# A gated recurrence and a mixture of experts on one core: who computes the convolution, and where the gates of two chunks stand

## What is computed

```python
xn = layernorm(x)
# branch 1: gated linear recurrence
xc = causal_depthwise_conv(xn, conv_w, conv_b)      # 4 taps along a sequence
r, i = sigmoid(xc @ W_r.T + b_r), sigmoid(xc @ W_i.T + b_i)
a = sigmoid(log_a) ** (8 * r)
h[t] = a[t] * h[t-1] + sqrt(max(1 - a*a, 0)) * (i * xc)[t]
attn = rmsnorm(h @ W_out.T) * gamma
# branch 2: 8 experts, one per token, at most 512 tokens each
probs = softmax(xn @ Wr);  e = argmax(probs)
slot = number of earlier tokens with the same e;  keep = slot < 512
y[token] = probs[e] * keep * (relu(xn[token] @ W1[e]) @ W2[e])
out = x + attn + y
```

## Time and profile before

| what | us |
|---|---|
| median of 3 runs | 165.67 (165.46 to 167.71) |
| the profiled execution, its own time | 165.59 |
| its span, first to last instruction | 163.8 |
| PE busy | 124.8 |
| DVE busy | 93.5 |
| ACT busy | 86.2 |
| POOL busy | 83.2 |

### The profile page before, as it was taken

The page is one execution under the profiler, slowest core; times in us unless marked ns, Lnnn a source line. Parts: engine busy times, 40 slices in busy tenths (PEclk is TensorE's granted clock), DMA queues, the critical chain, the costliest instruction groups (busy, mean ns, idle before and its releaser), DMA issues.

```text
span 163.8 us, 2058 instructions
## 1 busy us (share of the span) xinstructions
PE 124.8 (76%) x684; PEld 98.2 (60%) x684; DVE 93.5 (57%) x207; ACT 86.2 (53%) x197; POOL 83.2 (51%) x102
## 2 busy tenths in 40 slices
PE   5966999999995991699999739896979967941000
PEld 5956999836533890439659318694968956930000
DVE  4179300399898000861512410768948999299990
ACT  3047625014554840648685363999608958635650
POOL 7069640000477774377477876377765807560000
PEclk9997555579999999569999999999999999999555
DMA  4898699970011211011011111011110100116997
GB/s 133 231 270 315 268 356 342 399 318 2 16 48 36 54 58 48 18 49 49 16 52 48 48 48 48 16 50 49 49 46 21 33 16 32 42 58 183 327 301 214
DMA packets 14346, 19.27 MB, mean 118 GB/s; under 512 B 1664, under 2 KB 10112, under 8 KB 14336
## 3 DMA queue, kind: packets, MB, share of 16 engines
q1 hardware_dynamic: 9888, 13.63, 24.5%
q0 software_dynamic: 2048, 4.20, 8.7%
q10 hardware_dynamic: 2400, 1.32, 3.0%
HBM read 10.76 MB, written 8.39 MB: 117 GB/s over the span
## 4 chain that ended last, share of the span: by engine, by line
PE 40%; DVE 24%; DMA 8%; issue 8%; ACT 7%; another core or an unknown queue 6%; POOL 3%; POOLq 1%; SPq 0%; DVEq 0%; ACTq 0%
PE bank L495 8%; PE bank L427 7%; PE bank L385 7%; DVE xnT L869 5%; DMA x_tok<-in_x 4%; PE bank L395 4%; DVE xc L838 4%; PE bank L482 3%; DVE inp L865 3%; PE bank L416 3%; PE bank L484 2%; PE bank L483 2%; DVE dec L922 2%; DMA dec<-y_rows 2%
## 5 line engine op out<-in xcount | busy, mean ns | idle before, releaser
L357 POOL DMA_INDIRECT y_rows<-xn_tok,idx_out x32 | 37.1, 1159 | 25.2 <-DVE xn_tok L876 15.9
L350 POOL DMA_INDIRECT xn_tok<-xn_rows,idx_in x32 | 32.1, 1002 | 29.9 <-DVE idx_out L801 20.4
L618 ACT ACTIVATE h_sb<-bank 128x512 f32<-128x512 f32 x32 | 18.1, 596 | 25.7 <-PE bank L484 16.8
L495 PE MATMUL bank<-w_raw,h_sb 128*128 128x128 f32 x256 | 30.2, 275 | 0.1
L495 PEld LDWEIGHTS bank<-w_raw,h_sb 128*128 128x128 f32 x256 | 29.2, 192 | 0.2 <-issue 0.2
L482 PE MATMUL bank<-xg_hi,w_hi 128*128 128x512 f32 x32 | 14.0, 437 | 12.0 <-ACT h_sb L618 5.4
L427 PE MATMUL bank<-xc,par 128*128 128x512 f32 x32 | 17.2, 670 | 3.0 <-issue 2.8
L845 DVE TENSOR_TENSOR xg_lo<-bank,xg_hi 128x512 fp32r<-128x512 f32 x8 | 5.5, 688 | 18.6 <-ACT xg_hi L612 14.2
L876 DVE COPY xn_tok<-bank 128x512 f32<-128x512 f32 x7 | 4.8, 684 | 18.2 <-remote 11.3
L482 PEld LDWEIGHTS bank<-xg_hi,w_hi 128*128 128x128 f32 x32 | 6.1, 191 | 14.9 <-ACT h_sb L618 6.8
L427 PEld LDWEIGHTS bank<-xc,par 128*128 128x128 f32 x32 | 6.6, 214 | 12.0 <-issue 11.0
(11 more groups left out here) (111 smaller groups left out, 211.8 us busy)
## 6 DMA issues: line engine op xcount, KB each, us to landing
w_raw<-in_weights SPq DMA_DIRECT2D x8, 512.0 KB, 7.5
y_rows<-sca SPq DMA_DIRECT2D x4, 512.0 KB, 5.8
dec<-y_rows SPq DMA_DIRECT2D x8, 256.0 KB, 5.0
x_tok<-in_x SPq DMA_DIRECT2D x3, 512.0 KB, 9.4
xn_rows<-xn_tok SPq DMA_DIRECT2D x3, 512.0 KB, 3.5
out<-dec SPq DMA_DIRECT2D x4, 256.0 KB, 3.0
out<-dec ACTq DMA_DIRECT2D x4, 256.0 KB, 3.2
x_tok<-in_x SPq DMA_DIRECT2D x2, 256.0 KB, 5.4
```

Of the source, the lines that this page charges most:

```text
L350: g.indirect_dma_start(gathered[:, s * D:(s + 1) * D], None, xn_rows, bass.IndirectOffsetOnAxis(ap=idx_in[:, s:s + 1], axis=0)).then_inc(g ...
L357: g.indirect_dma_start(y_rows, bass.IndirectOffsetOnAxis(ap=idx_out[:, s:s + 1], axis=0), gathered[:, s * D:(s + 1) * D], None).then_inc(s ...
L495: last = mm(tile_of(e, s), h_sb[:, k * CAP + s * P:k * CAP + (s + 1) * P], w_raw[:, e, F + k * D:F + (k + 1) * D], start=(k == 0), stop=(k ...
L618: a(h_sb[:, k * CAP:(k + 1) * CAP], hbank[n % 3][:, :], ACT.Relu).then_inc(h_done, 1)
```

## The change

- PE no longer convolves and POOL no longer builds the diagonal matrices; `biased` is gone from ACT. DVE convolves all four chunks: chunks 0 and 1 before `untile(7)`, chunk 2 at the place of half 3, chunk 3 after `columns_rest(0)`.
- `gates(0)` stands on PE where the first half of conv 0 stood, before the counts, and `gates(1)` between counts and table. PE has nothing between the table and `turn(0)`. `gates(2)` and `gates(3)` stand in the turns of experts 0 and 1, and the turn of expert 2 has no gates.
- ACT computes Ln and loads the table set for exp before the routing, then the tanh of gates(0), then the exp of the logits, `lead(0)`, `lead(1)`, the tanh of gates(1), and decay(0) before `columns(0)`. decay(1) to decay(3) stand one turn earlier each.
- The three small instructions of DVE for `lna` move to behind `untile(7)`, ahead of the routing. gated and clip keep their turns but for those of chunk 2, which move from turn 3 to turn 2.

```diff
--- before.py
+++ after.py
...
-        diag = sb("diag", [P, TAPS, P])
...
-        PE_CONV = 3
...
-        def convolved(eng, n):
-
-            if n < PE_CONV:
-                eng.wait_ge(conv_act, n + 1)
-            else:
-                eng.wait_ge(conv_dve, TAPS * (1 + (n - PE_CONV + 1) // 2))
-
-        PE_AFTER_TABLE = "gates0"
+        def convolved(eng, c):
+
+            eng.wait_ge(conv_dve, TAPS * (c + 1))
+
         PE_AT = {5: "project0", 7: "project6 project7"}
-        PE_AFTER = {0: "gates1", 1: "gates2", 2: "gates3", 5: "project1 project2", 6: "project3 project4 project5"}
-        ACT_AT = {0: "decay0", 1: "decay1", 2: "decay2", 3: "decay3", 4: "scale1 scale2 scale3",
+        PE_AFTER = {0: "gates2", 1: "gates3", 5: "project1 project2", 6: "project3 project4 project5"}
+        ACT_AT = {0: "decay1", 1: "decay2", 2: "decay3", 4: "scale1 scale2 scale3",
                   6: "squares1 squares2", 7: "squares3 squares4 squares5 squares6 squares7"}
-        ACT_AFTER = {0: "gates1", 1: "gates2", 2: "gates3", 3: "scale0", 5: "squares0"}
+        ACT_AFTER = {0: "gates2", 1: "gates3", 3: "scale0", 5: "squares0"}
         DVE_AT = {4: "recur0", 6: "rows0"}
-        DVE_LATE = {0: "taps3", 1: "gated0 clip0", 2: "gated1 clip1", 3: "gated2 clip2 gated3 clip3",
+        DVE_LATE = {0: "gated0 clip0", 1: "gated1 clip1", 2: "gated2 clip2", 3: "gated3 clip3",
                     4: "recur1", 5: "recur2 recur3", 6: "rows1 rows2", 7: "rows3 rows4 rows5 rows6 rows7"}
         DVE_AFTER = {}
...
-            pool.wait_ge(par_in, 16)
-            pool.wait_ge(ident_done, 1)
-            for k in range(TAPS):
-                g.tensor_scalar(diag[:, k, :], ident[:, :], par[:, CONV_W + k:CONV_W + k + 1], 0.0, ALU.mult,
-                                ALU.add).then_inc(diag_done, 1)
...
-            def conv(n, first, last_tap):
...
-                for back in range(first, last_tap):
-                    if back == 0:
-                        ins = mm(bnk, diag[:, TAPS - 1, :], xnT[:, cols], start=True, stop=False)
-                    else:
-                        ins = mm(dst[:, :, back:], diag[:, TAPS - 1 - back, :], src[:, :, 0:L - back],
-                                 start=False, stop=(back == TAPS - 1))
-                if last_tap == TAPS:
-                    ins.then_inc(conv_mm, 1)
...
-                convolved(pe, 2 * c + i % 2)
+                convolved(pe, c)
...
-            conv(0, 0, 2)
+            gates(0)
...
-            conv(0, 2, TAPS)
-            conv(1, 0, 2)
+            gates(1)
...
-            conv(1, 2, TAPS)
-            conv(2, 0, TAPS)
 
             def turn(e):
                 pe.wait_ge(gather_in[e], 16 * ST)
-                if e == 0:
-                    pe.wait_ge(conv_act, PE_CONV)
-                else:
+                if e >= 1:
                     pe.wait_ge(xg_lo_done, e)
...
-            stages({0: PE_AFTER_TABLE}, 0, names)
             turn(0)
             up(0)
...
-            act.wait_ge(shift_done, 1)
-            a(shifted[:, :, :], shifted[:, :, :], ACT.Exp).then_inc(exp_done, 1)
-
-            def biased(n):
-                act.wait_ge(conv_mm, n + 1)
-                a(xc[:, n * HT:(n + 1) * HT], conv_bank[n % 2][:, :], ACT.Identity,
-                  bias=par[:, CONV_B:CONV_B + 1]).then_inc(conv_act, 1)
+            act.wait_ge(coef, 5)
+            a(lna[:, 4:5], lna[:, 3:4], ACT.Ln).then_inc(lna_act, 1)
+            nc.scalar.preload_act_table_set("exp_and_others")
...
-            biased(0)
+            gates(0)
+            act.wait_ge(shift_done, 1)
+            a(shifted[:, :, :], shifted[:, :, :], ACT.Exp).then_inc(exp_done, 1)
             lead(0)
             lead(1)
-            act.wait_ge(coef, 5)
-            a(lna[:, 4:5], lna[:, 3:4], ACT.Ln).then_inc(lna_act, 1)
-            nc.scalar.preload_act_table_set("exp_and_others")
-            biased(1)
-            biased(2)
-            gates(0)
+            gates(1)
+            decay(0)
             columns(0)
             relu(0)
...
+            def convolve(c):
+                cols = slice(c * TC, (c + 1) * TC)
+                src = xnT[:, cols].rearrange("d (s l) -> d s l", l=L)
+                dst = xc[:, cols].rearrange("d (s l) -> d s l", l=L)
+                for back in range(TAPS):
+                    k = CONV_W + TAPS - 1 - back
+                    if back == 0:
+                        ins = v.tensor_scalar(xc[:, cols], xnT[:, cols], par[:, k:k + 1],
+                                              par[:, CONV_B:CONV_B + 1], ALU.mult, ALU.add)
+                    else:
+                        dve.wait_ge(conv_dve, TAPS * c + back)
+                        ins = v.scalar_tensor_tensor(dst[:, :, back:], src[:, :, 0:L - back], par[:, k:k + 1],
+                                                     dst[:, :, back:], ALU.mult, ALU.add)
+                    ins.then_inc(conv_dve, 1)
+
+
+            for c in range(2):
+                transposed(dve, 2 * c)
+                transposed(dve, 2 * c + 1)
+                convolve(c)
             untile(7)
+            dve.wait_ge(lna_act, 1)
+            v.tensor_scalar(lna[:, 2:3], lna[:, 1:2], 1.0, None, ALU.add).then_inc(coef, 1)
+            dve.wait_ge(coef, 4)
+            v.reciprocal(lna[:, 3:4], lna[:, 2:3]).then_inc(coef, 1)
+            dve.wait_ge(lna_act, 2)
+            v.tensor_scalar(lna[:, 5:6], lna[:, 4:5], lna[:, 6:7], 4.0, ALU.add, ALU.mult).then_inc(coef, 1)
...
-            dve.wait_ge(lna_act, 2)
-            v.tensor_scalar(lna[:, 5:6], lna[:, 4:5], lna[:, 6:7], 4.0, ALU.add, ALU.mult).then_inc(coef, 1)
...
-            def convolve(first, last):
...
+                convolved(dve, c)
...
-            convolve(3, 4)
+            names = {"gated": gated, "clip": clip, "recur": recur, "rows": rows}
+            convolve(2)
             weights_rest(1)
-            taps_of_chunk(2)
             columns_rest(0)
+            convolve(3)
             for e in range(E):
```

More of the change, by code:

```diff
@@ L134, in rglru_moe_kernel @@
         tp = [bank[0], bank[1]]
-        conv_bank = [bank[2], bank[3]]
         gate = [bank[4], bank[5]]
@@ L166, in rglru_moe_kernel @@
         valued = sem("valued")
-        diag_done = sem("diag_done")
         coef = sem("coef")
@@ L192, in rglru_moe_kernel @@
         prob_done = sem("prob_done")
-        conv_mm = sem("conv_mm")
-        conv_act = sem("conv_act")
         conv_dve = sem("conv_dve")
@@ L802, in _ @@
                             ALU.add).then_inc(idx_done, 1)
-            dve.wait_ge(lna_act, 1)
-            v.tensor_scalar(lna[:, 2:3], lna[:, 1:2], 1.0, None, ALU.add).then_inc(coef, 1)
-            dve.wait_ge(coef, 4)
-            v.reciprocal(lna[:, 3:4], lna[:, 2:3]).then_inc(coef, 1)
             def weights_rest(e):
@@ L821, in _ @@
             v.tensor_tensor(prob[:, :], prob[:, :], keep[:, :], ALU.mult).then_inc(prob_done, 1)
-            dve.wait_ge(lna_act, 2)
-            v.tensor_scalar(lna[:, 5:6], lna[:, 4:5], lna[:, 6:7], 4.0, ALU.add, ALU.mult).then_inc(coef, 1)
-            taps = [0]
-            def convolve(first, last):
-                cols = slice(first * HT, last * HT)
-                src = xnT[:, cols].rearrange("d (s l) -> d s l", l=L)
-                dst = xc[:, cols].rearrange("d (s l) -> d s l", l=L)
-                for back in range(TAPS):
-                    k = CONV_W + TAPS - 1 - back
-                    if back == 0:
-                        ins = v.tensor_scalar(xc[:, cols], xnT[:, cols], par[:, k:k + 1],
-                                              par[:, CONV_B:CONV_B + 1], ALU.mult, ALU.add)
-                    else:
-                        dve.wait_ge(conv_dve, taps[0])
-                        ins = v.scalar_tensor_tensor(dst[:, :, back:], src[:, :, 0:L - back], par[:, k:k + 1],
-                                                     dst[:, :, back:], ALU.mult, ALU.add)
-                    ins.then_inc(conv_dve, 1)
-                    taps[0] += 1
             def columns_rest(e):
@@ L895, in rows @@
                 v.tensor_tensor(x_tok[:, cols], x_tok[:, cols], attn[:, cols], ALU.add).then_inc(sum_done, 1)
-            def taps_of_chunk(c):
-                convolve(2 * c, 2 * c + 2)
-            names = {"gated": gated, "clip": clip, "recur": recur, "rows": rows, "taps": taps_of_chunk}
-            convolve(3, 4)
+            names = {"gated": gated, "clip": clip, "recur": recur, "rows": rows}
+            convolve(2)
             weights_rest(1)
-            taps_of_chunk(2)
             columns_rest(0)
+            convolve(3)
             for e in range(E):
```

10 lines of the change are left out of this document (removed).

## The result

| | before | changed |
|---|---|---|
| median of 21 runs each, us | 166.07 (164.13 to 168.98) | 167.16 (165.97 to 171.14) |
| ratio, with 95% interval | 1 | 1.0217 (1.0163 to 1.0271) |
| profiled execution, its own time | 165.59 | 171.14 |
| busy PE, DVE, ACT, POOL | 124.8, 93.5, 86.2, 83.2 | 118.9, 100.2, 84.5, 81.3 |

The ratio leaves disturbed executions out, those about 1.5% above the fastest of their kernel or more; the means of the 19 and 15 runs left then differ by 1.0%, and the medians of all 21 by 1.1 us (0.7%). That the changed kernel is slower is clear; by how much, between 0.7 and 2.2%, is not. Its profiled execution was its longest of 21. So where a length matters a second pair of profiles from one chip (166.62 before, 168.47 changed) stands beside it; that 168.47, too, is 0.9 us above the median of its kernel on that chip.

A forecast was written before the change was run, and what follows sets the result against it. PE, the busiest engine, was taken to bound the kernel, with gathers and routing chain almost as much at turn(0). 165.6 + 2.6 (later gathers) - 6.4 (shorter turn 2) = 161.8 us; range 155.5 to 166.

The forecast's parts named there:

- The convolution on DVE: Opening, before the routing: DVE's copy of half 7 ends 0.8 us later, router(7) still on time; taken as 0 us.
- The price of gates(0) and gates(1) in the routing chain: Between routing and table: counts 1.8 us later, indices and every gather 2.6 us later; bounds 1.8 and 4.5.
- The cold clock and the moved stall: Table to relu(1): half clock costs up(0) 2.0 us, PE 4.1 later; the stall ends with the gathers, leaving only +2.6.
- Turn 2 loses 6.4 us: From turn(3) to turn(4): without gates(3) PE's turn is 6.4 us shorter; bounds 3.4 and 6.8.
- From turn(4) on both kernels do the same work: After turn 2: the work is the same in both kernels, so the 6.4 us gain was summed into the final time.
- POOL is not the bound: its scatters sat idle for 25.2 us in all: First reading of the profile: with 25.2 us of idle time at its scatters, POOL can follow if PE gets faster.
- The stall: Relu(1) and expert 0's eviction, at 66.15 and 66.17: PE's signals read as held until the sixteen gathers landed, not shown.
- Stall gone: Rival at relu(1): the stall belongs to one alignment of PE and gathers and goes away; 156 us, chance 0.30.
- Nothing gained: Rival: the stall keeps its length behind PE's work, 4.1 counts in full, the turn gives about 4; 165.7 us, chance 0.15.
- The slower rival: From PE's idle wait at 44 us the clock stays at half through up(0), down(0) and up(1); 169.6 us, chance 0.10.
- The collision: Rival in the opening: DVE's convolution waits for POOL's last two number tables, everything 2.2 us later; 164.0 us, chance 0.05.
- the bounds 1.8 and 6.8: Low side of the forecast's own range, 159.5 to 164: 1.8 us for DVE's delay, 6.8 for the shorter turn 2.

The follow-up runs named there:

- the run kept warm: Changed kernel with eight more matmuls of 512 columns, result unused, on PE between table and turn(0); 164.77 us, 1.02 (1.0111 to 1.0289) against the kernel before.
- wide down: Kernel before with down of experts 0 to 6 as four matmuls of 512 columns instead of sixteen of 128; 162.94 us (two runs), kernel before 166.90.
- the first group: Runs on one chip: kernel before 150.46 us; changed 1.0028; twelve gathers ahead, before 1.0284 and changed 1.0443; changed with gates(1) behind the table 0.9891.
- the second group: Runs on one chip: kernel before 164.65 us; DVE's convolution alone 0.9966; gates(0) and gates(1) behind the table 1.0139; changed with extra PE matmuls 1.02.

## Why the prediction was wrong

It said 161.8 us, 3.8 us faster; the median was 167.16, slower by 0.7% in the medians and 2.2% in the ratio. Point by point:

- **The convolution on DVE: right.** The copy of half 7 stood 0.80 us behind router(6), for 0.24 in the earlier trace rows, and the routing 3.46 us behind it in both. The kernel with this part alone was level (0.9966, 0.9874 to 1.0058).
- **The price of gates(0) and gates(1) in the routing chain: right, near the middle of its bounds.** From the routing's start to the counts it was 6.0 us in the second profile (6.8 in the first, where the granted clock was 0.60 from 34.00 to 37.45, for 0.73 in the second over nearly the same stretch) for 4.05 before; 1.8 was forecast to be added, and 1.9 (2.7) came. The table began 10.2 (11.0) us behind the routing's start for 7.4, so 2.8 (3.6) for the forecast 2.6. The first gather was 2.6 (3.0) us late. The wait of gates(1) for ACT was there, 0.63 us.
- **The cold clock and the moved stall: right.** up(0) cost 2.3 us more, for 2.0, and relu(1) came at 68.53, for 68.8. The warning of the Trainium skill that was weighed there ("TensorE: Matmul & The Clock Gate", Part 1), against idle gaps of PE, holds for this gap: the clock was 0.50 from 47.50 to 52.00, while PE waited, and through up(0). What it did not do is cost time: relu(1) was released with the gathers either way, and the run kept warm still lost 2.0%. The half clock behind the stall, 6.7 us in the earlier trace rows, did not come back in the first profile (1.00 from 69 to 80 us). In the second pair it did in part: 0.75 from 68.70 to 75.40, for 0.52 from 66.20 to 73.00 before.
- **Turn 2 loses 6.4 us: right for PE, wrong for the end.** The turn shrank from 14.4 to 8.3 us (15.9 to 7.9 in the second pair). The step that failed is "From turn(4) on both kernels do the same work", by which a gain of PE reached the end, and under it the first reading, "POOL is not the bound: its scatters sat idle for 25.2 us in all". That row was read wrongly. Of the 25.2, 9.6 are the gaps of 0.30 after 32 issues. The rest are six waits on evictions. The longest, 4.4 and 3.7 us, stand at experts 6 and 0, and only 3.35 at the scatter behind turn 2, so that at most 3.05 of the 6.4 could reach POOL there. Two of the six, 3.7 and 2.2 us, are behind evictions whose releaser the trace does not name, at 66.17 and 123.42. On the chip without the stall the changed kernel's POOL had no wait at all. In the second pair the turn's 8.0 us left 0.6 at that scatter, and in the two runs with gathers on time and a turn shorter by 3.8 us, 0.6 was left one expert further and nothing at the end. Without the 6.4 the sum is 165.6 + 2.6 = 168.2 in place of 161.8, against 168.47 in the second profile and 167.16 as a median.
- **The stall: read as it was, and not followed through.** The prediction placed its end by the sixteen gathers and was right: in eleven of the twelve profiles with sixteen gathers on the chips that have the stall, all but wide down, the eviction of expert 0 started 22.8 to 23.6 us after the first gather issue, whether PE was late, early or warm. But later evictions meet such a stall too, some behind the four gathers of an expert, as at 121.96; the trace of before had one at 123.42, 2.77 us. That a stall swallows what PE gains or loses ahead of it was applied once and not to turn 2.
- **The rivals.** Stall gone: that is the chip of the first group, but there the changed kernel was level (1.0028), not 10 us ahead, and its POOL issued without a wait. Nothing gained (165.7) came nearest to the median by its number, but not by its mechanism: the stall did not keep its length behind PE's work (DVE sat idle 6.16 us before it for 8.54), it moved with the gathers. The slower rival had the direction and named the wrong mechanism: no long cold spell, but late gathers with the gain lost. The collision came with the tiles POOL normalises, not with the number tables (2.21 us as before), and cost nothing that shows.
- **The range.** Its lower end was said to come from the bounds 1.8 and 6.8; they give 165.6 + 1.8 - 6.8 = 160.6, not 159.5. The measured median lay above the other end, so this slip changed nothing.

**What stays open.** Putting the gates behind the table keeps the first gather at 42.4 to 43.0, but gave 1.4% slower on one chip and 1.1% faster on another, so that this recovers the loss is not shown by time. It also means that the late first gather is not all: POOL's further waits move by several us from kernel to kernel (9.8 to 15.6 us on the chip of the second group), and no run separates them from the late start. The loss itself was 2.2% (0.7% in the medians), 0.5% and 0.3% on three chips, the last not clear of zero, and why it differs was not settled; on the chip without stalls the kernel before left no profile. What holds the signals was not found. No kernel was timed without its trace, so a part of the tracing in it is not excluded, and no other kind of gather was tried.

## What to carry to other kernels

An engine that is idle is not free to follow. Ask what its waits hang on, and before counting a gain in one turn look at when the other engines' next instruction could start: here POOL's next scatter stood behind its own eight issues, and its wait there, 3.35 us, was the most that a gain could be worth. Where one engine issues all gathers and scatters in a fixed order, time is its start plus its issues plus its waits, and work put in front of that start (2.6 us of gates here) can cost most of its length (3.4 us of delay alone cost 2.6, between 0.3 and 4.8 by the interval). Try a change of such an order on more than one chip.

## What the runs showed of the hardware

- **Signals of PE held while gathers are in flight.** Eleven of twelve profiles with sixteen gathers, on the chips that have the effect, show it at the same distance from the first issue, 1.9 to 2.6 us behind the end of the last one, with up to 8.8 us of idle time of DVE. ACT and DVE are released within 0.02 us of each other. In the twelfth, with `down` as 4 matmuls of 512 columns for 16 of 128, it did not occur at that place, and did at two later evictions (idle 3.03 and 5.10 us). The profile names no releaser, so that the gathers hold the signals is read from times alone.
- **It depends on the chip.** Three chips and the first measurement have it, 164.7 to 166.9 us for the kernel before; one chip has not, 150.5 us. The granted clock is no reason: the changed kernel's mean was 0.815 there and 0.813 in the second profile.
- **An indirect DMA of 128 rows costs POOL 0.94 to 1.0 us and a gap of 0.30 at best**, and up to 2.0 us at some places. 64 of them are 86 to 90 us of a kernel of 150 to 170.
